# Feed-forward products of two images at once in the quarters of TensorE's array

## The reference, cut to what matters

```python
h = relu(einsum('oc,bchw->bohw', w1, xn) + b1)      # block 0
ffn = einsum('oc,bchw->bohw', w2, h) + b2
return x_ifft + ffn

h1 = gelu(rf @ o1_w.T + o1_b, approximate=False)    # block 3, after linear attention
h2 = h1 @ o2_w.T + o2_b
return h2.transpose(0, 3, 1, 2) + bias0
```

## Time and profile before

| | us |
|---|---|
| median of 3 runs | 2815.92 (2815.85 to 2816.95) |
| the profiled execution | 2816.57 |
| its span, first to last instruction | 2814.8 |
| TensorE busy in the span | 2674.4 (95%) |
| VectorE busy | 1911.0 (68%) |
| ScalarE busy | 1361.5 (48%) |
| GpSimd busy | 66.4 (2%) |

### The profile page before, as it was taken

How to read it: one execution, slowest core, us unless ns; L and a number is a source line. 1 busy time by engine, 2 the same in 40 slices (tenths; PEclk the granted TensorE clock), 3 DMA queues, 4 the chain that set the end, 5 groups by cost and what they waited for, 6 DMA issues and landing times.

```text
span 2814.8 us, 111747 instructions
## 1 busy us (share of the span) xinstructions
PE 2674.4 (95%) x42486; PEld 2506.7 (89%) x42486; DVE 1911.0 (68%) x6167; ACT 1361.5 (48%) x2660; POOL 66.4 (2%) x145
## 2 busy tenths in 40 slices
PE   2999999999999999995999999999999999789999
PEld 1359999999999999995999999999999999779943
DVE  7766666666666666777666666666666667879943
ACT  1766664222233333456666622223333335689978
POOL 0000000000000000000000000000000000023300
PEclk9999999999999999997999999999999999889999
DMA  6640000222400000026800022231000002400023
GB/s 250 145 98 0 0 0 23 61 61 60 102 0 0 0 5 0 0 75 186 281 0 0 6 62 60 61 82 37 0 0 0 0 0 60 110 10 0 0 90 149
DMA packets 158388, 145.90 MB, mean 52 GB/s; under 512 B 22738, under 2 KB 146068, under 8 KB 154260
## 3 DMA queue, kind: packets, MB, share of 16 engines
q1 hardware_dynamic: 146432, 142.65, 17.3%
q10 hardware_dynamic: 11924, 2.90, 0.5%
HBM read 61.61 MB, written 50.33 MB: 40 GB/s over the span
## 4 chain that ended last, share of the span: by engine, by line
PE 94%; DMA 2%; DVE 1%; SPq 1%; issue 1%; ACT 1%; ACTq 0%; DVEq 0%; POOL 0%; POOLq 0%
PE banks L658 78%; PE banks L626 4%; PE banks L622 4%; PE banks L709 4%; PE banks L720 2%; DMA state<-x_in 1%; PE banks L706 1%; DMA res<-resid 1%; SPq L248 1%; DVE state L978 0%; PE banks L605 0%; DMA resid<-state 0%; ACTq L404 0%; DMA state<-resid 0%; ACT banks L540 0%
## 5 line engine op out<-in xcount | busy, mean ns | idle before, releaser
L658 PE MATMUL banks<-x_row,w_taps 128*64 128x124 f32 (+2 forms) x40640 | 2201.7, 270 | 11.1 <-DVE x_row L901 6.8
L658 PEld LDWEIGHTS banks<-x_row,w_taps 128*64 128x64 f32 x40640 | 2199.5, 135 | 13.2 <-DVE x_row L901 8.2
L901 DVE SCALAR_TENSOR_TENSOR x_row<-banks,sweep_nbias,biased_row 128x128 f32<-128x128 f32 x2032 | 713.3, 351 | 718.9 <-PE banks L658 705.7
L460 ACT ACTIVATE biased_row<-state,sweep_bias 128x256 f32 (+1 forms) x762 | 511.1, 671 | 1025.7 <-DVE state L904 591.9
L456 ACT ACTIVATE biased_row<-state,aff,gn_a 128x64 f32 (+1 forms) x1016 | 364.7, 430 | 183.2 <-DVE state L910 183.2
L904 DVE SCALAR_TENSOR_TENSOR state<-banks,sweep_nbias,biased_row 128x128 f32 (+1 forms) x1016 | 443.3, 436 | 0.2 <-issue 0.2
L910 DVE SCALAR_TENSOR_TENSOR state<-banks,sweep_nbias,biased_row 128x64 f32 (+1 forms) x1016 | 237.1, 275 | 0.2
L910 DVE SCALAR_TENSOR_TENSOR turn_ring<-banks,sweep_nbias,biased_row 128x64 f32<-128x64 f32 x1016 | 237.1, 275 | 0.0
L870 DVE TENSOR_TENSOR state<-banks,state 128x512 f32 x128 | 88.2, 689 | 99.1 <-PE banks L626 99.1
L626 PE MATMUL banks<-hid,ffn_w 128*128 128x512 f32 x256 | 134.7, 618 | 0.0
L709 PE MATMUL banks<-kv_w,res 128*128 128x256 f32 x512 | 132.2, 381 | 0.0
(11 more groups left out here) (115 smaller groups left out, 949.1 us busy)
## 6 DMA issues: line engine op xcount, KB each, us to landing
state<-turn_ring SPq DMA_DIRECT2D x512, 64.0 KB, 1.9
state<-x_in SPq DMA_DIRECT2D x16, 1024.0 KB, 20.9
resid<-state SPq DMA_DIRECT2D x64, 256.0 KB, 3.7
res<-resid SPq DMA_DIRECT2D x16, 1024.0 KB, 9.1
res<-resid SPq DMA_DIRECT2D x32, 512.0 KB, 5.5
resid<-state SPq DMA_DIRECT2D x16, 1024.0 KB, 11.7
out_y<-state SPq DMA_DIRECT2D x16, 1024.0 KB, 3.9
state<-resid SPq DMA_DIRECT2D x32, 256.0 KB, 9.2
```

Of the source, the lines that this page charges most:

```text
L460: nc.scalar.activation(as_cells(n, biased_row[:, k, :, :]), cells(n, slice(0, B), i, k, g), ACT.Identity, bias=sweep_bias[:, n:n + 1]).the ...
L658: last = nc.tensor.matmul(out_ps[blk, :, lo:hi], w_taps[:, n % 2, s, blk], x_row[c][src][:, :, s + lo:s + hi], start=at == 0, stop=at == T ...
L901: nc.vector.scalar_tensor_tensor(x_row[c][par][:, :, 2:2 + HALF], ps, nb, br, ALU.max, ALU.add).then_inc(row_ready[c], 1)
```

## The change

Each of the two products is made as two products of 64 rows by 64 columns, one for each half of the pixels, with only the diagonal blocks of the same weights. The first product of image b takes rows of half q and writes them to output partitions of half (q + b) % 2; so image 0 uses the two quarters on the array's diagonal and image 1 the two others. `hid` holds odd images with their halves exchanged, and the second product puts them back. `hid` has a buffer for each image, and the eight PSUM banks are one for each image and product. TensorE's order becomes: two images of first products, two images of second products (of the pair before), for all 16 chunks written out instead of looped. A semaphore is raised after the second half of each image. The scaling of image 0 stays on ScalarE, after the activation of image 1; that of images 1 to 3 moves to GpSimd, also written out, with a semaphore of its own. VectorE's instructions stay; it waits for the one semaphore or the other, and reads bank 4 + b.

```diff
-        hid = sb("hid", [P, 2, NT])
+        hid = sb("hid", [P, B, NT])
...
+        def half_of(q, b):
+            at = (q + b) % 2
+            return slice(at * C, (at + 1) * C)
...
+            def scale_x(layer):                     # GpSimd
+                base = B * CHUNKS * layer
+                pool.wait_ge(coefs_ready, 5 if layer else 1)
+                for j in range(CHUNKS):
+                    for b in range(1, B):
+                        pool.wait_ge(ffn_up_done, base + j * B + b + 1)
+                        xs = half_rows[:, j * 2 * CR:(j + 1) * 2 * CR, b, :]
+                        nc.gpsimd.tensor_scalar(xs, xs, a1[:, b:b + 1], cb[:, b:b + 1], ALU.mult,
+                                                ALU.add).then_inc(x_scaled_by_pool, 1)
...
-                    nc.scalar.activation(hid[:, b % 2, :], bank[b % 2], func, bias=ffn1_b[:, b:b + 1]).then_inc(hidden_ready, 1)
-                    xs = tile_of(j, b)
-                    nc.scalar.activation(xs, xs, ACT.Identity, scale=a1[:, b:b + 1], bias=cb[:, b:b + 1]).then_inc(x_scaled, 1)
+                    nc.scalar.activation(hid[:, b, :], bank[b], func, bias=ffn1_b[:, b:b + 1]).then_inc(hidden_ready, 1)
+
                 with act.Fori(0, CHUNKS) as j:
-                    for b in range(B):
-                        tile(j, b)
+                    tile(j, 0)
+                    tile(j, 1)
+                    xs = tile_of(j, 0)
+                    nc.scalar.activation(xs, xs, ACT.Identity, scale=a1[:, 0:1], bias=cb[:, 0:1]).then_inc(x_scaled, 1)
+                    tile(j, 2)
+                    tile(j, 3)
...
                 def up(j, b):
-                    nc.tensor.matmul(bank[b % 2], ffn1_s[:, b, :], tile_of(j, b),
-                                     start=True, stop=True).then_inc(ffn_up_done, 1)
+                    for q in range(2):
+                        src, dst = slice(q * C, (q + 1) * C), half_of(q, b)
+                        last = nc.tensor.matmul(bank[b][dst], ffn1_s[src, b, src],
+                                                half_rows[src, j * 2 * CR:(j + 1) * 2 * CR, b, :], start=True, stop=True)
+                    last.then_inc(ffn_up_done, 1)
+
+                def down(j, b):
+                    pe.wait_ge(hidden_ready, base + j * B + b + 1)
+                    if j:
+                        pe.wait_ge(ffn_added, base + (j - 1) * B + b + 1)
+                    for q in range(2):
+                        src, dst = half_of(q, b), slice(q * C, (q + 1) * C)
+                        last = nc.tensor.matmul(bank[B + b][dst], ffn2_w[src, layer, src], hid[src, b, :], start=True, stop=True)
+                    last.then_inc(ffn_down_done, 1)
+
+                for j in range(CHUNKS):
+                    for first in (0, 2):
+                        up(j, first)
+                        up(j, first + 1)
+                        if first:
+                            down(j, 0)
+                            down(j, 1)
+                        elif j:
+                            down(j - 1, 2)
+                            down(j - 1, 3)
+                down(CHUNKS - 1, 2)
+                down(CHUNKS - 1, 3)
...
-                        dve.wait_ge(x_scaled, j * B + (base + b + 1))
+                        if b == 0:
+                            dve.wait_ge(x_scaled, j + (CHUNKS * layer + 1))
+                        else:
+                            dve.wait_ge(x_scaled_by_pool, j * (B - 1) + ((B - 1) * CHUNKS * layer + b))
                         dve.wait_ge(ffn_down_done, j * B + (base + b + 1))
                         xs = tile_of(j, b)
-                        nc.vector.tensor_tensor(xs, bank[2 + b % 2].rearrange("p (r w) -> p r w", w=WH), xs,
+                        nc.vector.tensor_tensor(xs, bank[B + b].rearrange("p (r w) -> p r w", w=WH), xs,
                                                 ALU.add).then_inc(ffn_added, 1)
```

More of the change, by code:

```diff
@@ L164, in build_program @@
         x_scaled = sem("x_scaled")
+        x_scaled_by_pool = sem("x_scaled_by_pool")
         ffn_down_done = sem("ffn_down_done")
@@ L367, in tails @@
                                         rkv[:, k, :].rearrange("p (g h) -> p g h", h=HQ), ALU.mult).then_inc(tails_ready, 1)
+            def scale_x(layer):
[7 more added lines that the diff above has]
+                                                ALU.add).then_inc(x_scaled_by_pool, 1)
+            scale_x(0)
             for b in range(B):
@@ L373, in _ @@
                     tails(b, j * B + b)
+            scale_x(1)
         @block.scalar
```

## The result

The changed kernel takes 2747.65 us (median of 4 runs, 2747.18 to 2751.44), the kernel before 2815.89 us beside it: a ratio of 0.9762, interval 0.9745 to 0.9779. It is 68 us faster; the forecast was 2748 us. The profiled execution is the slowest of the four (2751.44, span 2749.6).

A forecast was written before the change was run, and what follows sets the result against it. The prediction took TensorE to bound both networks; -23.6 us in network 1 and -43.9 us in network 2 made -67.5 us, from 2815.9 to 2748 us, with a range of 2740 to 2804 us.

The forecast's parts named there:

- Four quarters at once: TensorE in both networks: with all four quarter products at once, two images cost 0.86 us and a chunk 3.44 us.
- The loading of the written-out code: TensorE's 16 written-out chunks in each network: code loading costed at nothing; a guessed 8 stops of 2 us would be 16 us.
- Rival 2: Both networks: only two quarters run at once, 6.88 us a chunk, 14 us gained, 2802 us; chance 0.12.
- Network 1: First 16-chunk stretch: VectorE becomes the bound at 5.77 us a chunk, ending at 156.9 instead of 180.5, -23.6 us.
- First add as before at 64.37: Start of network 1: VectorE's first add keeps its time, hanging on the same first product, activation and second product.
- the DMA share: Stores in network 1: the share would rise from 0.66 to 0.84, leaving the 6.0 us to the sweeps.
- Network 2: Second 16-chunk stretch: ScalarE becomes the bound at 4.52 us a chunk, last activation at 2763.7 instead of 2807.59, -43.9 us.
- the price: GpSimd's scaling of 512 elements in both networks: 1.0 us each, 3.0 us a chunk, hidden behind 4.52 and 5.77.
- rival 5: Both networks: GpSimd's scaling costs over 2.44 us, 4.9 us by L364's rate, losing 236 us, 3052 us; chance 0.08.
- rival 4: TensorE's clock falls to 1.2 GHz where it pauses: 2766 us, or 2804 with both networks low; chance 0.09.
- rival 3: GpSimd and VectorE take turns: network 1 at 8.8 us a chunk, network 2 at 5.8, 2816 us; chance 0.07.

The follow-up runs named there:

- the doubled run: The changed kernel with GpSimd making every scaling once more into a spare buffer ahead of the one in place: 2750.34 us, 0.9772 of the kernel before.

## Why the prediction was right

**The bound before** was TensorE: whole products in the new order still cost 6.87 us a chunk, and GpSimd's relief alone did nothing.

**Four quarters at once**, which no row of before showed, hold: four records in progress, and 3.43 us a chunk where TensorE is the bound, against my 3.44. The loading of the written-out code, which I put at nothing, shows no cost in that run either: TensorE is busy 20.00 of 20 us. Rival 2 gave 2802, and the run with two quarters, which is what it describes, came to 2806.

**Network 1** was forecast at -23.6 us and gave -24.1. Two small errors offset. "First add as before at 64.37" was wrong: it came at 64.82, released by ScalarE's scaling (the row above), which now stands behind two activations instead of one. And an image costs 1.43, not 1.444 us. TensorE's 5.2 of 5.77 us came out as 35.12 of 40, or 5.0 of 5.72. I put the DMA share at 0.84; it is 0.77, and the 6.0 us to the sweeps stay.

**Network 2** was forecast at -43.9 us and gave -45.4. ScalarE's chunk is 4.44 instead of 4.52 us: its activations give way after 0.58, not 0.59 us, and the load holds it 1.30, not 1.35 us. That is 0.08 x 15 = 1.2 us.

**GpSimd** takes 0.77 us where I took 1.0, between the ends of 0.53 and 1.9. Under rival 5 the text allowed for about what a filling does (0.53); the scaling costs half as much again. Up to 1.5 us the price costs 1.4 us in all, as the doubled run shows. Rival 5 itself rested on L364's 0.70 us. All 64 of these, in both kernels, ran beside VectorE's L1032 (now L1064), so what one costs by itself stays open.

**The clock** (rival 4) stayed at 2.4 GHz through the chunks of both networks, also in network 1, where TensorE is busy 35.12 of 40 us. It is low in the first 2 us of network 2, as before, and the first activation comes 2.0 us after the first product there, against 2.1. In network 1 it falls at 154.4 us, when TensorE's last product has ended (151.1) and only VectorE's instructions are left, 0.61 and 0.81 us apart as all along. **The shared port** (rival 3) is refuted by the doubled run for these instructions; its sum took VectorE's bare adds at 2.8 us a chunk, though the text above it has 3.0.

**That the median meets the forecast to 0.4 us** is partly luck. The networks gave 2.0 us more than forecast, and the rest takes it back.

**What the sum left out** is scatter between the networks. They save 69.5 us, the profiled span only 65.2. From the end of network 1 to the first product of network 2 are 2515.1 us here and 2510.8 before, and in the ten other kernels profiled, which differ in nothing there, this stretch varies by 7 us. Between the networks the clock is at 1.2 GHz for 101.9 us in all here and for 93.6 us before; at half the speed the 8.3 us more would cost at most 4.2 us (an estimate). In the twelve kernels profiled, the shortest such stretch (2508.8 us) has the least time at the lower clock (82.0 us) and the longest (2515.8 us) the most (102.6 us). One of the low stretches inside the sweeps, which the kernel before does not have, with TensorE busy throughout:

```profile
1594.40:1597.80 3.40, 3.40 (x40) 3.40 (x38) 1.39 (x7) 0.51 (x1) 0.00 (x0) 0.56 0.22 57
```

What sets how often this happens was not tried, and that it is the whole of the difference is not shown. The medians, 68.2 us apart, agree with the networks' sum to 1.3 us.

## What to carry to other kernels

When the bound is lifted, work out the next one of each stretch by itself: the same change made VectorE the bound of one network and ScalarE of the other, and moving work to GpSimd was worth 34 us in one and nothing in the other. Small products that fill only a block diagonal can share the array in pairs of images, but only if the second image takes the other quarters; splitting alone gains nothing. Take an engine's pace from the starts of its instructions where it runs without waits: a handful of such distances gave this forecast to within 2 us for each network.

## What the runs showed of the hardware

- Four float32 products of 64x64 weights and 512 columns run at once in the four quarters: a chunk's eight image products (four images, two products each) take 3.43 us against 6.87 us as whole products. Two in two quarters gain nothing over one whole product.
- GpSimd scales 512 elements (one input, multiply and add with a value for each partition) in 0.77 us, the next starting 0.75 us later, beside a VectorE that is busy 90% of the time.
- A table load of 1.28 us came back in every pass of ScalarE's loop in network 2 (gelu and scaling), 16 times, and once in all when that loop was written out, though the functions alternate in the same way. The loop of network 1 (relu and scaling) had none.
- Statistics that wait for the add just ahead on VectorE start 0.82 us after it; with another add between, two instructions start 0.60 us apart.
